# Graph attention and experts on one core: a ring of four for the edge-counting one-hots, low parts by VectorE, second attention layer in two spans

## The reference

```python
def gat_layer(x, W, a_src, a_dst, bias, src, dst, heads, out_c):
    h = (x @ W).reshape(n, heads, out_c)
    e = leaky_relu(al_s[src] + al_d[dst], 0.2)   # al_s, al_d: h times a_src, a_dst, summed over c
    ex = exp(e - segment_max(e, dst)[dst])
    alpha = ex / segment_sum(ex, dst)[dst]
    return segment_sum(h[src] * alpha, dst) + bias

g = elu(gat_layer(layernorm(x), W1, ..., heads=8, out_c=96))
x = x + gat_layer(g, W2, ..., heads=1, out_c=768)
x = x + experts(layernorm(x))      # 4 groups of 8 experts, 2 groups and 4 experts per node
```

## Time and profile before

| what | value |
|---|---|
| median of 3 runs | 1727.28 us (1722.03 to 1732.57) |
| the profiled execution | 1734.71 us, its span 1733.0 us |
| TensorE clock granted over the span | 0.912 of full speed |
| busy: TensorE, VectorE, ScalarE, GpSimd | 1427.9, 1137.1, 729.1, 515.6 us |
| edge counting, 75 to 363 us | 288 us |
| second layer, 669 to 757 us | 88 us |

### The profile page before, as it was taken

How to read it: one execution, slowest core, us unless ns; L and a number is a source line. 1 busy time by engine, 2 the same in 40 slices (tenths; PEclk the granted TensorE clock), 3 DMA queues, 4 the chain that set the end, 5 groups by cost and what they waited for, 6 DMA issues and landing times. The chain is left out here.

```text
span 1733.0 us, 30177 instructions
## 1 busy us (share of the span) xinstructions
PE 1427.9 (82%) x7585; PEld 1162.6 (67%) x7586; DVE 1137.1 (66%) x1618; ACT 729.1 (42%) x1096; POOL 515.6 (30%) x557
## 2 busy tenths in 40 slices
PE   5777777858787776879951999999999999899895
PEld 5354544543332235879951899899999999888895
DVE  5367878769999995655666655444454635675762
ACT  2355454424444451321111554444454535565650
POOL 0000000000235221211211445455454545444450
PEclk8698998859999996889975999999999999999995
DMA  3200000051221223222333978867777877998956
GB/s 150 115 16 8 16 16 8 15 203 58 84 64 53 66 70 122 69 64 92 98 109 109 309 191 190 225 154 164 178 194 187 222 159 193 236 288 218 234 100 207
DMA packets 99194, 227.50 MB, mean 131 GB/s; under 512 B 14825, under 2 KB 51433, under 8 KB 98901
## 3 DMA queue, kind: packets, MB, share of 16 engines
q1 hardware_dynamic: 76100, 146.16, 25.9%
q0 software_dynamic: 20864, 74.68, 20.8%
q10 hardware_dynamic: 2192, 6.20, 0.9%
HBM read 167.03 MB, written 56.05 MB: 129 GB/s over the span
## 5 line engine op out<-in xcount | busy, mean ns | idle before, releaser
L872 PE MATMUL ps_o<-prob,h_head 128*97 128x512 f32 (+1 forms) x480 | 190.4, 536 | 52.8 <-DVE prob L813 52.8
L1803 POOL DMA_INDIRECT sum_dram<-y,to_index x93 | 164.2, 1766 | 221.9 <-DMA sum_dram<-y,to_index 174.4
L2056 PE MATMUL ps_h<-e_hi,e_xt_hi 128*128 (+1 forms) x546 | 197.0, 361 | 6.2 <-DVE e_xt_lo L1948 5.3
L1948 DVE TENSOR_TENSOR e_xt_lo<-ps_xt,e_xt_hi 128x768 fp32r<-128x768 f32 x92 | 88.1, 958 | 170.4 <-ACT e_xt_hi L1896 168.5
L2035 PE MATMUL ps_y<-e_hi,e_ht_hi 128*128 (+1 forms) x546 | 191.7, 351 | 2.0 <-DVE e_ht_lo L1988 2.0
L872 PEld LDWEIGHTS ps_o<-prob,h_head 128*97 128x97 f32 x480 | 74.4, 167 | 168.9 <-issue 88.8
L2056 PE MATMUL ps_h<-e_hi,e_xt_lo 128*128 (+1 forms) x546 | 186.9, 342 | 0.0
L2056 PE MATMUL ps_h<-e_lo,e_xt_hi 128*128 (+1 forms) x546 | 186.7, 342 | 0.0
L1960 DVE TENSOR_TENSOR e_lo<-raw,e_hi (+1 forms) x192 | 178.8, 952 | 8.8 <-ACT e_hi L1904 7.4
L2035 PE MATMUL ps_y<-e_hi,e_ht_lo 128*128 (+1 forms) x546 | 184.6, 338 | 0.0
L2035 PE MATMUL ps_y<-e_lo,e_ht_hi 128*128 (+1 forms) x546 | 183.9, 337 | 0.0
(11 more groups left out here) (333 smaller groups left out, 3037.7 us busy)
## 6 DMA issues: line engine op xcount, KB each, us to landing
raw<-in_ew SPq DMA_DIRECT2D x192, 384.0 KB
w_room<-rel_dram SPq DMA_DIRECT2D x16, 640.0 KB, 4.9
b_all<-in_eb SPq DMA_DIRECT2D x32, 192.0 KB
al_src<-al_dram SPq DMA_DIRECT2D x1, 5120.0 KB, 14.4
xs<-in_x SPq DMA_DIRECT2D x1, 3840.0 KB, 17.9
x_in_t<-in_x SPq DMA_DIRECT2D x10, 384.0 KB, 3.6
sum_dram<-x SPq DMA_DIRECT2D x10, 384.0 KB, 4.0
table<-xf SPq DMA_DIRECT2D x10, 384.0 KB, 2.3
```

What stands on the lines that cost most here:

```text
L872: turn = nc.tensor.matmul(ps_o[u][0:C1 + 1, c, 0:WID[c]], h_head[:, u, t, :], prob[:, t % 2, 512 * c:512 * c + WID[c]], start=(t == 0), st ...
L1803: nc.gpsimd.indirect_dma_start(s.sum_dram.ap(), bass.IndirectOffsetOnAxis(to_index[:, w:w + 1], 0), y[:, w, :], None, bounds_check=ROWS - ...
L2056: summed = nc.tensor.matmul(ps_h[:, 0:HID], a, b[:, bass.ds(e % 2, 1), c * HID:(c + 1) * HID] .rearrange("p o m -> p (o m)"), start=(c == ...
```

## The change

In the edge counting (`transform_and_count`):
- `HOTS` is 4 instead of 2, for `one_src` and `one_dst`; `away` keeps two slots.
- The low part of x is made by VectorE (`rest_x(t)`, after the one-hots of tile t and ahead of `largest(t - 1)`) and written over `x_t` itself (`s.x_lo` is the same memory as `s.x_t`). GpSimd's subtraction goes.
- To make room, `al_src` is 1250 wide instead of 1280 (its broadcast load then has eight rows of 5000 bytes per partition instead of one of 40960), `mask` has one slot instead of two, and `dst_f` is freed after stage 1.

In the second layer:
- Scores, exponents and products are made for destinations 0 to 511 and 512 to 1279 apart (`SPANS`), in an order written by hand (`UNITS`). Each unit has 512 or 768 columns. There are three slots for scores, and the counts are loaded unit by unit, again into three slots.
- `rel` and `bend` are made for tiles 0 to 3 after four scans, and for the rest at the end; the rows for the first span leave while the scans of the others run.
- The low parts of g are made by VectorE (`rest_g`), beside `rest_h`; `turn_over(t)` is `rest_h(t)` and then `rest_g(t + 2)`. `TURNS` says ahead of which unit each stands.

```diff
@@ transform_and_count
-        HOTS = 2
+        HOTS = 4
-        al_src = sb("al_src", [P, H1, NP])
-        xt_lo = sb("xt_lo", [P, 2, D], F32R)
-        mask = sb("mask", [P, 2, NP], BF16)
+        al_src = sb("al_src", [P, H1, N])
+        mask = sb("mask", [P, NP], BF16)
...
-                for t in range(NT):
-                    pool.wait_ge(xhi_made, t + 1)
-                    nc.gpsimd.tensor_tensor(xt_lo[:, t % 2, :], ...).then_inc(xlo_made, 1)
...
+                def rest_x(t):
+                    dve.wait_ge(xhi_made, t + 1)
+                    nc.vector.tensor_tensor(s.x_lo[:, t], s.x_t[:, t], xt_hi[:, t % 2].bitcast(F32),
+                                            ALU.subtract).then_inc(xlo_made, 1)
+
                 one_hots(0)
+                rest_x(0)
                 for t in range(1, NT):
                     one_hots(t)
+                    rest_x(t)
                     largest(t - 1)
                 largest(NT - 1)
@@ second_layer
+        SPLIT = 4
+        EDGE = SPLIT * P
+        WIDE = NP - EDGE
+        SPANS = ((0, EDGE), (EDGE, WIDE))
+        UNITS = ([(0, t) for t in range(7)] + [(1, t) for t in range(4)]
+                 + [(0, 7), (1, 4), (1, 5), (1, 6), (0, 8), (1, 7), (0, 9), (1, 8), (1, 9)])
+        TURNS = {0: 2, 4: 3, 8: 4, 11: 5, 14: 6, 17: 7, 19: 8}
...
@@ SyncE
+                spread_rows(0)
+                spread_rows(1)
+                for n in range(COUNTS, 2 * NT):
+                    sp.wait_ge(made, n - COUNTS + 1)
+                    load_count(n)
@@ GpSimd
-                for t in range(NT):
-                    pool.wait_ge(ghi_made, t + 1)
-                    nc.gpsimd.tensor_tensor(g_lo[:, t % 2], ...).then_inc(glo_made, 1)
@@ ScalarE
+                for n in range(2 * NT + 1):
+                    if n < 2 * NT:
+                        exp(n)
+                    if n - 1 in TURNS and n > 1:
+                        keep_h(TURNS[n - 1])
+                keep_h(NT - 1)
@@ VectorE
+                rest_g(0)
+                rest_g(1)
                 dve.wait_ge(al_spread, 1)
-                for t in range(4):
+                for t in range(SPLIT):
                     largest(t)
...
+                relate(0, SPLIT)
+                for t in range(SPLIT, SPLIT + 2):
                     largest(t)
+                turn_over(0)
...
+                for m in range(2):
+                    make_score(m)
+                for m in range(2 * NT):
+                    if m and m in TURNS:
+                        turn_over(TURNS[m])
+                    if m + 2 < 2 * NT:
+                        make_score(m + 2)
+                    make_prob(m)
+                rest_h(NT - 1)
```

More of the change, by code:

```diff
@@ L907, in second_layer @@
         junk = work[:, 3 * NP:4 * NP].bitcast(BF16).rearrange("p (r n) -> p r n", r=2)
-        steep, flat = work[:, 0:NP], work[:, NP:2 * NP]
-        score = work[:, 2 * NP:4 * NP].rearrange("p (r n) -> p r n", r=2)
-        count = sb("count2", [P, COUNTS, NP], U16)
+        near = sb("rows_near", [P, 2, EDGE])
+        far = work[:, 0:2 * WIDE].rearrange("p (r n) -> p r n", r=2)
+        steep, flat = (near[:, 0, :], far[:, 0, :]), (near[:, 1, :], far[:, 1, :])
+        score = work[:, 2 * NP:2 * NP + SCORES * WIDE].rearrange("p (r n) -> p r n", r=SCORES)
+        count = sb("count2", [P, COUNTS, WIDE], U16)
         best = sb("best2", [P, NT])
@@ new lines, in make_score, with make_prob @@
+                def make_score(n):
+                    span, t = UNITS[n]
+                    if n >= SCORES:
+                        dve.wait_ge(made, n - SCORES + 1)
+                    dve.wait_ge(rows_in[span], 32)
+                    nc.vector.scalar_tensor_tensor(score[:, n % SCORES, 0:SPANS[span][1]], flat[span], bend[:, t:t + 1],
+                                                   steep[span], ALU.add, ALU.max).then_inc(scored, 1)
+                def make_prob(n):
+                    span, t = UNITS[n]
+                    at, width = SPANS[span]
+                    dve.wait_ge(exped, n + 1)
+                    dve.wait_ge(count_in[n % COUNTS], 16 * (n // COUNTS + 1))
+                    used = NP * t + at + width - NP * (NT - KD)
+                    if used > 0:
+                        dve.wait_ge(glo_made, -(-used // D))
+                    nc.vector.scalar_tensor_tensor(s.prob2[:, t, at:at + width], score[:, n % SCORES, 0:width], 1.0,
+                                                   count[:, n % COUNTS, 0:width], ALU.min, ALU.mult).then_inc(made, 1)
@@ L1048, in _ @@
+                for t in range(SPLIT + 2, SPLIT + 4):
                     largest(t)
[L1049 to L1056 removed]
@@ L1070, in _ @@
+                for t in range(SPLIT + 4, NT):
+                    largest(t)
+                relate(SPLIT, NT)
+                turn_over(2)
+                for m in range(2):
[7 more added lines that the diff above has]
+                rest_h(NT - 1)
             @block.tensor
@@ L1071, in _, with turn_rows @@
             def _(pe):
+                def turn_rows(first, end, to):
+                    for b in range(first, end):
+                        last = nc.tensor.transpose(to[0:2, (b - first) * P:(b - first + 1) * P], rel[:, b, :],
+                                                   s.ident[:, :])
+                    last.then_inc(rel_turned, 1)
                 for t in range(NT):
@@ L1080, in _ @@
                 for t in range(NT):
-                    if t == EARLY:
-                        pe.wait_ge(step, chain)
-                        for c, (at, width) in enumerate(PARTS):
-                            for b in range(at // P, (at + width) // P):
-                                last = nc.tensor.transpose(ps_all[0:2, c, b * P - at:(b + 1) * P - at], rel[:, b, :],
-                                                           s.ident[:, :])
-                            last.then_inc(rel_turned, 1)
+                    if t == 1:
+                        pe.wait_ge(al_kept, 1)
+                        pe.wait_ge(rel_made, 1)
+                        turn_rows(0, SPLIT, ps_c)
                     pe.wait_ge(glo_made, t + 1)
```

179 lines of the change are left out of this document (86 added, 93 removed).

## The result

The changed kernel takes 1680.91 us, the median of 4 runs (1675.64 to 1687.69); the kernel before took 1726.63 us (1722.03 to 1732.57) in the runs beside it. The ratio is 0.9728, with an interval of 0.9695 to 0.9761: 45.7 us saved, where 52 were forecast. The forecast of 1675 us is 6 us too low, and the result is inside the range of 1660 to 1697.

A forecast was written before the change was run, and what follows sets the result against it. The prediction held that the two-slot ring paced the edge counting, with VectorE and TensorE waiting for each other. Savings of 46 us there and 6 in the second layer, off the profiled 1734.7, gave a median of 1675 us, range 1660 to 1697.

The forecast's parts named there:

- The counting: Edge counting stage: 46 us saved, 44 of it in eight cycles from tile 2 to 9, at 22.3 instead of 27.8.
- The ring sets this pace: Edge counting: two slots yield two pairs per round of about 3.1 us; four slots would give 0.8 us a pair.
- 22.1 us: Edge counting, nine-pair tile: length of the chain of ScalarE and TensorE in turn, with pairs at ScalarE's 1.36 us.
- The small terms of the counting: Edge counting: tiles 0 and 1 save 2.5 us; one subtraction ahead of the last scans loses 0.9 us.
- wrong if the pairs still start every 1.5 us: Sign set for the edge counting's profile: pairs still starting every 1.5 us would prove the forecast wrong; 1.36 was expected.
- VectorE's 22.2 us: Edge counting, nine-pair tile: VectorE's limit from one-hots 9.3, subtraction 0.88, mask 0.95 and eight scans 11.1 us.
- The clock: Edge counting, TensorE: idle ahead of a tile shrinks from 4.7 to 1 to 2 us; granted clock 1.00 from tile 2.
- TensorE keeps falling to half speed: Rival, edge counting: slow pairs take 1.70 us against 1.36, costing 15 us in all, 1690 us; chance 0.13.
- GpSimd's subtraction: Edge counting: moving it to VectorE removes nine stretched scans (14.4 us), adds 8.8; 5.6 us if the ring gave nothing.
- The second layer: Second layer: 6 us saved, ending at 750.5 instead of 757.0, with the first score 7.4 us earlier.
- The second layer gains nothing: Rival, second layer: VectorE's waits behind exponentials and the lost 6 us make 10 to 12 us more, 1687; chance 0.08.
- The ring does not do what it says: Rival, edge counting: slots help only inside a tile, the stage keeps 5.6 and the layer 6, 1715 us; chance 0.03.

The follow-up runs named there:

- e9: The changed kernel with a ring of three pairs of one-hots (HOTS 3) instead of four: 1690.22 us.
- e1: The changed kernel with a ring of two pairs of one-hots (HOTS 2) instead of four: 1712.52 us.
- e5: The changed kernel with the low part of x subtracted by GpSimd again instead of VectorE: 1680.77 us.
- e2: The edge counting of the changed kernel joined to the second layer of the kernel before: 1689.12 us, ratio to before 0.9767.
- e7: The changed kernel with ScalarE writing the high part of h2 one exponential earlier in the second layer: 1678.05 us.
- e3: The edge counting of the kernel before joined to the second layer of the changed kernel: 1722.8 us, ratio to before 0.9969.
- e10: The changed kernel with the low part of g in the second layer subtracted by GpSimd again: 1682.43 us.
- e4: The changed kernel without TensorE's third product in each pair (sources 1024 to 1279, whose edges go uncounted): 1678.46 us.
- e6: The changed kernel with ScalarE's h_ext of a tile and next split of x moved behind the next tile's one-hots: 1675.12 us.
- e8: The changed kernel with the edits of e6 and e7 together and five slots instead of three for the second layer's counts: 1668.8 us.

## Why the prediction was right, and where its steps were not

- **The counting: 46 us forecast, 40.0 measured.** The step that failed is the sentence "The ring sets this pace". It does not: 1.54 us is TensorE's loop. Already before, a pair for which nothing was late (194.19) started at that distance. I then let pairs go at ScalarE's 1.36 and summed 22.1 us. The chain I named is the right one; with 8 pairs at 1.54 instead of 9 at 1.36 in it, it is 23.6. TensorE's closing products show the eight cycles from the second to the tenth falling from 222.5 us (117.41 to 339.91) to 187.7 (115.22 to 302.89): 34.8 saved, where I had 44. That the sum still came out only 6 too high is in part luck: the two small terms below made up 3.6 of these 9.
- **The small terms of the counting.** The stage up to the second closing product, tiles 0 and 1, gave 3.2 us (forecast 2.5). The tail, from the last closing product to the end of the stage, gave 2.0 where I had lost 0.9: with four slots VectorE is further ahead of TensorE in the last tile too.
- **The test "wrong if the pairs still start every 1.5 us"** came out against me though the time fell. The ring works through VectorE's lead over TensorE, not through the pace of a pair. The test was drawn from the wrong mechanism.
- **VectorE's 22.2 us** was its busy time without a wait. It does wait, because the last one-hots need slots: 23.0 by the formula that e9 bore out. Its waits for `ps_c` over the stage are 30.7 us; 15 were forecast, 64.1 was before.
- **The clock.** The gap ahead of a tile was forecast at 1 to 2 us and is 1.46 to 1.62 from tile 2 on. Stretches at half speed in tiles 2 to 9 fell from eight, one in each, to one (198 to 201 us), so "1.00 from tile 2 on" was not quite so. The rival *TensorE keeps falling to half speed* fell with this; in e1, with gaps near 4 us, there is one in each of these tiles again. The rival had its price wrong as well: it charged 0.34 us for each slow pair, and with three slots (e9) tiles with a slow stretch were no longer than those without.
- **GpSimd's subtraction.** The 5.6 us that I gave it if the ring brought nothing measured 7.8 (e1, with what makes room). Its working was off too: the trace of before has seven scans of 3.05 or 3.06 us, not nine, and the first four one-hots took 3.93 instead of 1.93. Of the 7.8, 6.3 lie in the eight cycles from the second closing to the tenth. That it was inside other limits with the full ring was right (1.1, e5).
- **The second layer: 6 us forecast, 7.9 in this trace** but 4 to 7 over all: the mean of seven executions with the new code is 81.4 (80.3 to 82.2), and the old code took 88.2 (before) and 85.3 (e2). Half of the difference between those two lies ahead of the first score, where TensorE's granted clock over the first 9 us was 0.50 in the one and 0.62 in the other; the other half was not traced to a cause. The new code shows the same step: 28.4 and 28.3 us to the first score in the two executions that began at 0.62 (the changed kernel and e7), 29.3 to 30.1 in the seven with this order of VectorE that began at 0.50. The claim that the early start is spent later holds: the first score is 8.2 earlier (7.4 forecast; some 7 where both began at the same clock), and from there the layer takes 51.9 (52.3 by my sum) instead of 51.6, or 50.2 in e2. Behind the first score the new order gains nothing. Waits at the turns 3 to 8 were none, 0.83, 0.84, 0.62, 0.84 and 0.23 (about 1.0 forecast at each of 3 to 7); the one for counts 1.62 (2.4). Scores of 512 and 768 columns follow at 0.67 and 0.93 and products, where a score comes next, at 0.72 and 0.98, not 0.62 and 0.91. From the first score to turn 7 the scores and products took 29.4 us instead of 27.2 and the waits 5.1 instead of 8.1, so that 51.9 comes so near to 52.3 is in part two misses that cancel.
- **Other rivals.** *The second layer gains nothing* fell with e3. *The ring does not do what it says* fell with e5. One-hots kept their fast form (540 to 555 ns each).

The wait for the fourth unit's counts on VectorE in the changed kernel, and TensorE's longest gap for `g_lo`, both forecast at their places:

```profile
667.04 0.69 DVE L1090 SCALAR_TENSOR_TENSOR prob<-work,count 128x512 f32<-128x512 f32 x1 [1.62 <-DMA count<-count_dram]
```

```profile
678.67 0.44 PE L1154 MATMUL ps_h<-w_hi,g_hi 128*128 128x384 f32 x1 [2.61 <-DVE g_lo L1059]
```

## What to carry to other kernels

A ring between two engines need not change the pace of what passes through it to be worth much: count how far ahead the producer can finish, and what it can begin then. Before the pace of a loop is put down to a wait, look for one of its turns in which nothing was late; its start-to-start time is the floor. And sum every chain that comes near the longest: here ScalarE's 23.6 us and VectorE's 23.0 lay side by side, so that in these tiles a repair of one gave only the distance to the other. A slot more can also take the price off a stall: with two slots each stretch at half clock cost 1.0 us, with three nothing.

## What the runs showed of the hardware

- Six matmuls of 1.08 us in a loop with two waits on TensorE come every 1.54 us when nothing is late. The trace shows 0.30 of it as idle, since it models the end of a pair at 1.24; the closing product that follows a pair outside the loop starts at 1.08, so the loop's own part is 0.46. At half speed this part is not added: the pairs then follow without an idle gap (12 matmuls in e1, 30 in e9), and in e9 five pairs in a row, the first of them slow, still take 1.556 us each.
- GpSimd's subtraction of two SBUF operands stretched, by 1.5 to 1.6 us, each of these operations of VectorE when it ran beside it: the scan, the one-hots (one of 2108 ns in e5), the score (e10). `h_lo`, which takes one operand from PSUM, ran in 0.95 beside GpSimd's subtraction at 668.85 in e10. The Trainium skill (SBUF — State Buffer, Who interferes with whom) says that a VectorE instruction with at most one SBUF input, outside the two-port modes, does not contend with GpSimd, that one with two SBUF inputs contends with a GpSimd instruction that reads SBUF, and that the shared ports are an exclusive lock. The runs agree: the stretch is near the 1.8 to 2.1 us that GpSimd's subtraction takes, and only 0.78 us for the score at 669.71 in e10, which began when 1.0 of it was left. Which mode the one-hots run in is not shown.
- The longer TensorE's idle gap ahead of a tile, the more of the tiles 2 to 9 had a stretch at half speed (granted 0.50). With gaps near 4.7 us (before; 3.1 ahead of tile 9) and 4 us (e1) every one had, with 2.4 us (e9) six of eight. With 1.5 us it was one of eight in the changed kernel, e4 and e5, two in e2 and e10 and none in e7; with 0.8 to 1.0 us (e6, e8) none.
